# Message rows of a graph kernel: the bias added by VectorE between its statistics, ScalarE's rectification in place

## What is computed

```python
def _layernorm(x, axis=-1, eps=1e-05):
    m = jnp.mean(x, axis=axis, keepdims=True)
    v = jnp.var(x, axis=axis, keepdims=True)
    return (x - m) / jnp.sqrt(v + eps)

def _hconv(x, src, dst, ew, w1, b1, w2, b2, g, b):
    h = jax.nn.relu(x @ w1 + b1)              # the message rows
    msg = ew[:, None] * h[src]
    agg = jax.ops.segment_sum(msg, dst, num_segments=x.shape[0])
    h = agg @ w2 + b2
    return jax.nn.relu(_bn(h, g, b))

h = _hconv(_layernorm(x), src, dst, edge_weight, c1_w1, c1_b1, ...)
```

## Time and profile before

| | us |
|---|---|
| median of 3 runs | 5399.52 |
| lowest, highest | 5396.0, 5408.83 |
| the profiled execution | 5405.47 |
| its span in the profile | 5403.7 |
| `combine_message` in it, from SP's first transfer to SP's first of the next stage | 2650.29 to 2738.93 |

### The profile page before, as it was taken

How to read it: one execution, slowest core, us unless ns; L and a number is a source line. 1 busy time by engine, 2 the same in 40 slices (tenths; PEclk the granted TensorE clock), 3 DMA queues, 4 the chain that set the end, 5 groups by cost and what they waited for, 6 DMA issues and landing times. The chain is left out here.

```text
span 5403.7 us, 82597 instructions
## 1 busy us (share of the span) xinstructions
PE 3775.3 (70%) x19299; PEld 3215.4 (60%) x19306; DVE 2017.6 (37%) x5468; ACT 1956.5 (36%) x4823; POOL 3105.3 (57%) x2684
## 2 busy tenths in 40 slices
PE   3666666666657499999766666766556666665789
PEld 2555555555545388888655565666455566665567
DVE  6444444455547511111222222223422222224555
ACT  3222333332334222222343333333633333334543
POOL 5888888888840033333257777775177777772110
PEclk8777888888888799999877778788777777788899
DMA  8777766776670666666433333332133333331000
GB/s 248 88 88 88 88 88 88 88 87 88 87 186 25 171 184 185 185 184 184 119 103 102 102 102 101 103 101 78 64 103 101 103 102 102 103 101 34 24 16 25
DMA packets 373213, 569.87 MB, mean 105 GB/s; under 512 B 68039, under 2 KB 297099, under 8 KB 371188
## 3 DMA queue, kind: packets, MB, share of 16 engines
q0 software_dynamic: 210224, 344.84, 33.5%
q1 hardware_dynamic: 161652, 206.40, 12.4%
q10 hardware_dynamic: 1232, 17.43, 0.8%
HBM read 398.97 MB, written 169.49 MB: 105 GB/s over the span
## 5 line engine op out<-in xcount | busy, mean ns | idle before, releaser
L763 POOL DMA_INDIRECT A<-h_rows,segment_sum_idx x1568 | 1540.3, 982 | 699.3 <-issue 527.0
L800 PE MATMUL bank<-A 128*128 128x128 f32 x7808 | 1286.5, 338 | 758.7 <-PEq L70 757.9
L800 PEld LDWEIGHTS bank<-A 128*128 128x128 f32 x7808 | 1220.9, 249 | 824.5 <-issue 824.0
L448 POOL DMA_INDIRECT node_sums<-T,scattered_sum_idx x760 | 1181.6, 1555 | 241.6 <-issue 219.8
L779 ACT ACTIVATE A<-A,segment_sum_edge 128x256 f32<-128x256 f32 x1568 | 668.0, 496 | 1178.6 <-DMA A<-h_rows,segment_sum_idx 1178.6
L550 PE MATMUL bank<-X,T 128*128 x1952 | 624.1, 477 | 99.5 <-PEq L70 96.3
L544 PE MATMUL bank<-T 128*128 128x128 f32 x1952 | 346.1, 333 | 399.2 <-PEq L70 399.2
L828 DVE TENSOR_TENSOR T<-T,bank 128x256 f32 x488 | 205.3, 421 | 1104.0 <-DVEq L70 1104.0
L550 PEld LDWEIGHTS bank<-X,T 128*128 128x128 f32 x1952 | 456.9, 246 | 196.1 <-issue 121.1
L544 PEld LDWEIGHTS bank<-T 128*128 128x128 f32 x1952 | 305.5, 236 | 415.1 <-issue 410.7
L1641 POOL DMA_INDIRECT x_rows<-A,expert_ffn_ring_out x104 | 164.4, 1581 | 500.7 <-DMA x_rows<-A,expert_ffn_ring_out 258.5
(11 more groups left out here) (328 smaller groups left out, 4267.4 us busy)
## 6 DMA issues: line engine op xcount, KB each, us to landing
T<-in_L_ffn_W SPq DMA_DIRECT2D x52, 1024.0 KB
A<-in_L_ffn_W SPq DMA_DIRECT2D x52, 1024.0 KB
T<-src_lanes SPq DMA_DIRECT2D x196, 128.0 KB, 3.3
A<-h_rows,segment_sum_idx POOLq DMA_INDIRECT x1568, 2.8
A<-node_sums SPq DMA_DIRECT2D x36, 512.0 KB, 6.4
node_sums<-A ACTq DMA_DIRECT2D x2, 6528.0 KB, 30.6
h_rows<-A SPq DMA_DIRECT2D x50, 256.0 KB, 2.1
node_sums<-T,scattered_sum_idx POOLq DMA_INDIRECT x784, 4.0
```

Of the source, the lines that this page charges most:

```text
L448: pool.indirect_dma_start(c.sum_dram[at % COPIES], bass.IndirectOffsetOnAxis(ap=idx[:, h % LR, j:j + 1], axis=0), msg[:, h % LR * G + j, : ...
L763: pool.indirect_dma_start(msg[:, h * G + j, :], None, c.h_dram, bass.IndirectOffsetOnAxis(ap=idx[:, h, j:j + 1], axis=0)).then_inc(landed[ ...
L800: mm = pe.matmul(acc[s][:, k * P:(k + 1) * P], msg[:, h * G + j, k * P:(k + 1) * P], hot[:, s, j, :], start=(j == 0), stop=(j == G - 1))
```

## The change

POOL's part of the stage, the matrix of ones and the bias in three bf16 parts are gone, and with them PE's first wait and its L1868 matmul. DVE now adds the bias: `add(j)` takes the finished product, reads the bank and the bias, writes `c.A` (L1878 of the changed kernel, two instructions of one tile), and then frees the bank and lets ACT rectify `c.A` in place (L1819). DVE's statistics of the first two parts (16 tiles) are still taken ahead of all blocks; those of the other 34 tiles are dealt out, `PER` = 3 tiles ahead of each `add`, so they end with block 11. `begin(n)` follows the last tile of part n at once, ahead of that block's `add` (blocks 3, 7 and 11); ACT takes the root at the start of the next block's step, and `close(n)` follows that block's `add`. The roots of the first two parts both stand ahead of `normed(0)`.

```diff
@@ act
             def normed(j):
                 s = j % 2
                 for n, (lo, hi) in enumerate(PARTS):
                     if lo == j * 2:
-                        root(act, go, done, c.rstd[:, lo:hi])
                         act.wait_ge(stats_ready[n], 1)
...
             def relu(j):
-                s = j % 2
-                take(act, prod[s])
-                act.sem_inc(col_free[s], 1)
-                act.activation(c.A[:, j * 2:j * 2 + 2, :].rearrange("p t d -> p (t d)"), out[s][:], ACT.Relu).then_inc(stored, 1)
-                act.sem_inc(out_free[s], 1)
-
+                r = c.A[:, j * 2:j * 2 + 2, :].rearrange("p t d -> p (t d)")
+                take(act, added)
+                act.activation(r, r, ACT.Relu).then_inc(stored, 1)
+
+            for n in range(2):
+                root(act, go, done, c.rstd[:, PARTS[n][0]:PARTS[n][1]])
             normed(0)
             normed(1)
             turn_copy(0)
             for j in range(NJ):
+                for n, step in begun_at.items():
+                    if step == j - 1:
+                        root(act, go, done, c.rstd[:, PARTS[n][0]:PARTS[n][1]])
                 if j + 2 < NJ:
                     normed(j + 2)
@@ pe
-                pe.matmul(out[s][:], one[:], pieces[:].rearrange("p t d -> p (t d)"), start=True, stop=False, skip_group_check=True)
                 for q in range(2):
                     for k in range(KD):
                         mm = pe.matmul(out[s][:, q * D:(q + 1) * D], col[s][:, k, q * P:(q + 1) * P], w[:, k, :],
-                                       start=False, stop=(k == KD - 1), skip_group_check=True)
+                                       start=(k == 0), stop=(k == KD - 1))
                 mm.then_inc(prod[s], 1)
 
             pe.wait_ge(*w_ready)
-            pe.wait_ge(one_made, 2)
@@ dve
+            def add(j):
+                s = j % 2
+                take(dve, prod[s])
+                dve.sem_inc(col_free[s], 1)
+                for q in range(2):
+                    dve.tensor_tensor(c.A[:, j * 2 + q, :], out[s][:, q * D:(q + 1) * D], bias[:], ALU.add).then_inc(kept, 1)
+                take(dve, kept, 2)
+                dve.sem_inc(out_free[s], 1)
+                dve.sem_inc(added, 1)
...
+            close(1)
+            dve.wait_ge(b_in, 16)
+            at = first
+            for j in range(NJ):
+                for t in range(at, min(at + PER, NB)):
...
+                    stat_tile(dve, c, t)
+                    for n, step in begun_at.items():
+                        if t == PARTS[n][1] - 1:
+                            assert step == j
+                            begin(n)
+                at = min(at + PER, NB)
+                add(j)
+                for n, step in begun_at.items():
+                    if step == j - 1:
+                        close(n)
```

More of the change, by code:

```diff
@@ L1770, in run @@
     def run(block, sb, sem):
-        bias, one = sb("bias", [P, D]), sb("one", [P, P], BF16)
-        pieces, left, third, part = sb("pieces", [P, 2, D], BF16), sb("left", [P, D]), sb("third", [P, D], BF16), sb("part", [P, D])
-        mask = sb("mask", [P, 3])
+        bias = sb("bias", [P, D])
         col = [sb(f"col{s}", [P, KD, BLK]) for s in range(2)]
@@ L1779, in run @@
         row_ready, turned, col_ready, row_free, col_free = (pair(sem, n) for n in ("row_ready", "turned", "col_ready", "row_free", "col_free"))
-        prod, out_free, one_made = pair(sem, "prod"), pair(sem, "out_free"), sem("one_made")
-        made = sem("made")
+        prod, out_free = pair(sem, "prod"), pair(sem, "out_free")
+        kept, added = sem("kept"), sem("added")
+        PER = 3
+        first = PARTS[1][1]
+        begun_at = {n: -(-(hi - first) // PER) - 1 for n, (lo, hi) in enumerate(PARTS) if n >= 2}
+        assert all(step + 1 < PARTS[n][0] // 2 - 2 for n, step in begun_at.items())
         @block.sync
@@ L1793, in _ @@
             sp.wait_ge(h_out, 16 * NJ)
[L1795 to L1817, removed]
         @block.scalar
@@ L1888, in close, with begin @@
                 dve.sem_inc(stats_ready[n], 1)
-            for n, (lo, hi) in enumerate(PARTS):
+            def begin(n):
+                dve.drain().then_inc(v, 1)
+                take(dve, v)
+                begin_stats(dve, go, c, v, slice(*PARTS[n]))
+            def add(j):
[7 more added lines that the diff above has]
+                dve.sem_inc(added, 1)
+            for n in range(2):
+                lo, hi = PARTS[n]
                 dve.wait_ge(rows_in[n], 16)
@@ L1893, in _ @@
                     stat_tile(dve, c, t)
[L1894 to L1899, removed]
+                    if n == 1 and t == lo + 2:
+                        close(0)
+                begin(n)
[4 more added lines that the diff above has]
+                for t in range(at, min(at + PER, NB)):
+                    for n, (lo, hi) in enumerate(PARTS):
+                        if t == lo:
+                            dve.wait_ge(rows_in[n], 16)
+                    stat_tile(dve, c, t)
+                    for n, step in begun_at.items():
+                        if t == PARTS[n][1] - 1:
+                            assert step == j
+                            begin(n)
+                at = min(at + PER, NB)
[3 more added lines that the diff above has]
+                        close(n)
     stage(nc, run, "combine_message")
```

## The result

| | kernel before | changed kernel |
|---|---|---|
| median of 13 runs each | 5406.17 us | 5416.69 us |
| lowest, highest | 5396.0, 5409.38 | 5411.44, 5421.07 |
| span of the profiled execution | 5403.7 | 5412.5 |
| the stage in it, SP's first load to its load for the next stage | 88.64 | 100.75 |

The ratio is 1.0021, with a 95% interval of 1.0013 to 1.003: about 11 us slower. It lies inside the 0.3%, and yet clear of no change. The stage alone grew by 12.1 us. The median of the kernel before was 5399.52 us in the three runs on which the prediction builds, and is 5406.17 us with ten more.

What follows compares the result with a forecast made beforehand. PE bounds the kernel before; after the change, a ring through PE, DVE and ACT. Start -0.5, rings +5.3, begins +2.6, end +0.7 sum to +8.1 us: 5399.5 + 8.1 = 5407.6 us, range 5396 to 5417.

Steps and rivals of the forecast that it cites:

- three begins: begin_stats ahead of the additions of blocks 3, 7 and 11, delaying them; +2.6 us together, including three roots of 0.2.
- What bounds the kernel now: Steady part of combine_message: PE bounds at 2.37 us a block, just above a two-block ring of 4.58, 2.29 for one.
- The hop over DVE is added to the ring: Product-to-product chain of two blocks through PE, DVE, ACT: 5.57 us, 2.79 a block, becomes the bound; 11 rings, +5.3 us.
- without the 0.21 of the ones, 2.08: Ring: product's first load to its consumer falls from 2.29 to 2.08 us once the ones matmul is gone.
- So I take 2.13: Ring: load-to-addition time assumed, near the lower end of 2.08 to 2.35 us, as PE idles ahead of its product.
- The clock falls: Slow-side rival: PE's idle drops its clock to the 1.2 GHz level, +23 us from the first begin, 5430 us; chance 0.14.
- DVE's dealt-out statistics cost nothing: Steady blocks: two additions with their wait and three statistics take 2.07 us, hidden in a block of 2.79.
- 0.72 is spare: DVE's slack at a begin: against the 2.25 us of begin_stats, it leaves the first addition late by 1.5.
- The even blocks decide: Cost of the begins: block 24 is last, so the even blocks' lateness counts, 2.1 us plus three roots of 0.2.
- The start: Stage start: POOL's work goes but the second part's root precedes the first norm; PE 0.4 us earlier, sum -0.5 us.
- PE stays bound: Rival: a shorter ring leaves PE the bound at 2.16 us a block, -9.3 us, 5390 us; chance 0.14.
- DVE binds: Rival: DVE binds as well after a begin, with uneven gaps of 2.2 against its 2.07; +11 us, 5411 us; chance 0.10.

Runs made afterwards that it cites:

- e2: Changed kernel without begin_stats, root and finish_roots of the last three parts (those tiles normed with old values); stage 95.52 us, ratio 0.9997.
- e3: Kernel before without POOL's work, PE's first wait and the ones matmul, so without the bias; stage 79.39 us, ratio 0.9979.
- e1: Changed kernel with ACT's rectification of a block one step later in its stream; stage 89.45 us, ratio 0.9963; run again 89.09 us, 0.9985.
- e5: Changed kernel with rectification one step later and without begin_stats, root and finish_roots of the last three parts; stage 79.60 us, ratio 0.9984.
- e4: Changed kernel with a bf16 matmul of ones with zeros put back ahead of each product; stage 100.99 us, ratio 1.0002.
- e6: Changed kernel with the second part's root moved behind turn_copy(0), no longer ahead of normed(0); stage 97.36 us, ratio 1.0017.
- e8: Changed kernel with begin_stats of the last three parts on POOL, root and finish_roots one block later; stage 96.41 us, ratio 1.0025.
- e7: Changed kernel with later rectification, later second root, and last three begin_stats on POOL (root, finish_roots one block later); stage 76.86 us, ratio 0.9986; again 76.48, 0.9976.
- after_again: Changed kernel unaltered, timed and profiled again on the chip where the kernel before takes 5401 us; stage 100.33 us, ratio 1.0021.

## Why the prediction was off

It said 5407.6 us, 8.1 more than before and within what can be told from no change; the stage grew by 12.1 and the runs by about 11. Of the 9.1 us between 5407.6 and the median of 5416.69, 6.65 lie in the base: 5399.52 us from three runs, 5406.17 from thirteen. The mechanism was right, and so was the sign of the 8.1, which the forecast called too small to tell; at 1.0021 it can be told. What is short by 4.0 us is the sum for the stage. By its own steps, with the rectifications of blocks 2 and 24 as the marks:

| step | said | measured |
|---|---|---|
| start, to block 2's rectification (the hop of the end counted here) | -0.5 + 0.7 = +0.2 | +0.7 |
| 11 rings | +5.3 | +6.65 (`e2`: 61.88 against 55.23) |
| three begins | +2.6 | about +2.4 |
| the clock behind a begin | 0, a rival if it lasts | about +1.8 |
| blocks 20 and 24 | - | +0.5, cause open |
| sum | +8.1 | +12.1 |

- **What bounds the kernel now: right.** The bound of before was PE with a ring just behind it. `e3` shows how near: with PE relieved, the blocks fell by 0.12 on average and not by 0.21.
- **"The hop over DVE is added to the ring": the mechanism right, shown by `e1` and `e5`, one term too small.** 1.11, 0.53, 0.98 and 0.82 were measured as 1.12, 0.53, 0.98 and 0.83. The step that failed is "without the 0.21 of the ones, 2.08", and with it "So I take 2.13": loads to additions took 2.24. `e3` shows where the 0.11 come from. It has no hop over DVE, and from the first load to the rectification it takes 2.19 us at an idle PE, not 2.08; the 0.05 for DVE added on top were right. The 0.21 are what the ones matmul costs a PE that is always busy. In a ring in which PE starts from idle its removal gives 0.14 (`e3`), and putting it back costs 0.15 (`e4`). The sentence that the figure doesn't enter the sum was thus wrong too: it entered through the 2.08. Eleven rings make 1.2 us of it.
- **The clock at nothing: the other step that failed, and the larger one.** "The clock falls" was put as a case that either lasts or doesn't occur. It fell for one product behind one begin, and twice in `e6`, at 1.7 to 1.8 us each. The warning was in the idle of 2.1 at each begin that the prediction itself names; it was priced at nothing in the sum. That `message_rows` holds its clock with gaps of 0.4 says nothing about gaps of 2.3. The Trainium skill, page "TensorE: Matmul & The Clock Gate", section "A second HAM failure mode: psum-queue depth-cycling", blames frequent short pauses; here those, 1.32 once in a ring, left the clock at 1.00 (the window from 2712 to 2730), and only the single long ones let it fall, in some of the cases.
- **"DVE's dealt-out statistics cost nothing": right** (`e5`, also at 2.17 a block). **The begins: the size right, by two errors that cancel.** It took the blocks to be 2.79 apart, each like the other. A ring of two fixes only the sum of two gaps, and they came at 2.17 and 3.54 from the first block on (rectifications at 24.48, 26.65 and 30.19 us into the stage; 2.16 and 3.55 in turn all through `e2`). Blocks 3, 7 and 11 lie behind the short one, where DVE has nothing spare. So "0.72 is spare" failed, and the first begin came through whole, 2.28 late and not 1.5. But the gap behind it is the long one, and PE makes up 1.5 in it and not 0.6. That left 0.8 at block 4 and 1.0 at block 6, against the 0.9 that was said. "The even blocks decide" was right.
- **The start: right that nearly nothing comes of it** (17.60 for 17.77 us, 0.17 in place of 0.4), and why: the second root. `begin_stats` of the second part was taken at 2.1 us; up to the root it took 2.49 (2660.03 to 2662.52), with a wait of 0.52 ahead of its second instruction. `e3` and `e6` price what the root hid at 4.5 to 6.4 us.
- **The end: right.** ACT waits 1.10 for the last addition, the hop that was priced at 1.11 (in the table it is in the first line), and store and barrier are unchanged.
- **PE stays bound: excluded.** DVE binds: excluded in the steady steps; it binds only at the begins.

Open is why the stage's gain doesn't go over whole in two kernels. On the chip of 5401 us the runs of the changed kernel and of `e6` lie where their stages put them, within 2 us. `e8` lies some 5 us above its stage, `e7` 4 to 5. Both have POOL work in the stage; in their profiles the part from SP's next weight load (after `message_rows`) to the end is 1508.3 and 1510.9 us, against 1506.2 in `after_again` and 1505.6 before. On the other chip `e7` shows no such loss. One profile each doesn't settle it, and no run was made for it.

## What to carry over

Before work is moved off the busiest engine, write down the ring behind it: with double buffers, one block's chain through all engines, divided by two, is a second bound, and a hop of 1.1 us that is added to it counts in full, however idle the engine that makes it. Here the hop was free once the engine that waits for it did its next block's work first (`e1`, stage 100.8 to 89.4). Take the price of an instruction in the ring from rows where its engine starts from idle, not from rows where it is always busy: the ones matmul was worth 0.21 us in the one case and 0.14 in the other. And when a startup dependency is removed, look at what stands next in the same queue: here the second root gave back nearly the whole of it.

## What the runs showed that I had not expected

PE's granted clock fell to its 1.2 GHz level behind an idle of 2.27 to 2.34 us, but not each time. In the changed kernel it fell behind the second begin (2.33 and 2.34 in its two profiles) and not the first (2.31 in both); in `e6` behind both; in both profiles of `e1` behind the third and not the second, each with an idle of 2.33 or 2.34. A product then took up to 3.65 us (`e6`) in place of 1.97. It stayed up behind 2.17 and 2.20 in `e4`, and behind the third begin of the changed kernel and of `e6` (1.84 and 1.85). In `e2` and `e5`, where PE is never idle for longer than 1.4 us once the products run, it stayed at 1.00 behind the slow start. What decides between two idle times of the same length, no run here shows.
